# TensorE's increments and the waits on its products in the edge stage of a graph attention kernel

## The reference

```
h          = einsum('ni,hio->hno', layernorm(x), W)
edge_attn  = leaky_relu(attn_src[:, src] + attn_dst[:, dst], 0.2)
exp_attn   = exp(edge_attn - max(edge_attn))
attn_sum   = segment_sum(exp_attn, dst)
out        = segment_sum(exp_attn / (attn_sum[dst] + 1e-10) * h[:, src], dst)
x          = x + layernorm(x) + out
```

## Time and profile before

| | us |
|---|---|
| median of 3 runs | 1986.72 |
| lowest and highest | 1985.87, 1988.36 |
| the profiled execution, its own time | 1983.17 |
| its span | 1981.4 |

### The profile page before, as it was taken

One profiled execution on the slowest core, in us unless ns is written; L12 is line 12 of the kernel. 1 busy time (PEld: TensorE's weight loads), 2 busy tenths in 40 slices (PEclk: granted clock), 3 DMA queues, 4 the chain that ended last, 5 costly groups with the idle time before them and its releaser, 6 DMA issues.

```text
span 1981.4 us, 28027 instructions
## 1 busy us (share of the span) xinstructions
PE 1518.3 (77%) x6733; PEld 1113.7 (56%) x6733; DVE 1177.7 (59%) x3449; ACT 775.5 (39%) x2346; POOL 1213.1 (61%) x1197
## 2 busy tenths in 40 slices
PE   3927777777777777777777777673968999999975
PEld 2714444444444444444444444442848999999963
DVE  5746666666666666666666666668983444333338
ACT  2624444444444444444444444432622233223326
POOL 4066666666666666666666666645364776666757
PEclk9956666666666666766656666766559999999987
DMA  6544444444444444444444444432856878877876
GB/s 184 164 120 115 120 112 113 115 117 118 112 115 114 117 118 110 114 115 117 118 111 115 114 119 114 115 79 80 252 168 184 226 212 210 213 210 203 217 170 200
DMA packets 166686, 284.19 MB, mean 143 GB/s; under 512 B 31760, under 2 KB 93285, under 8 KB 166373
## 3 DMA queue, kind: packets, MB, share of 16 engines
q0 software_dynamic: 62256, 143.99, 30.5%
q1 hardware_dynamic: 101908, 137.90, 21.9%
q10 hardware_dynamic: 2368, 0.52, 0.2%
HBM read 240.97 MB, written 42.16 MB: 143 GB/s over the span
## 4 chain that ended last, share of the span: by engine, by line
PE 63%; DVE 18%; issue 8%; DVEq 3%; another core or an unknown queue 3%; POOL 2%; DMA 1%; ACT 1%; ACTq 0%; POOLq 0%; SPq 0%
PE bank L1057 29%; PE bank L1198 10%; PE bank L1210 10%; DVE region L1518 4%; PE bank L1046 3%; PE bank L1082 3%; PE bank L990 2%; DVE z L1471 2%; DVE region L1516 2%; DVEq L494 2%; PE bank L1043 2%; POOL region L925 1%; DVE z L1478 1%; DVE z L1483 1%
## 5 line engine op out<-in xcount | busy, mean ns | idle before, releaser
L895 POOL DMA_INDIRECT region<-node_rows,region x832 | 790.5, 950 | 483.7 <-issue 222.7
L1057 PE MATMUL bank<-region 128*128 128x264 f32 x1664 | 746.7, 597 | 84.5 <-DVE region L1518 81.3
L1057 PEld LDWEIGHTS bank<-region 128*128 128x128 f32 x1664 | 440.5, 290 | 224.2 <-issue 138.4
L1518 DVE TENSOR_TENSOR region<-region,bank 128x264 f32 x728 | 311.5, 428 | 354.3 <-PE bank L1057 269.0
L748 ACT ACTIVATE neg_max<-bank 128x1 f32<-128x1 f32 x104 | 17.8, 171 | 723.1 <-PE bank L1082 593.6
L1504 DVE TENSOR_TENSOR region<-region,bank 128x512 f32<-128x512 f32 x416 | 265.9, 681 | 7.2 <-ACT bank L755 4.8
L738 ACT ACTIVATE region<-iota_row,region 128x128 f32<-128x128 f32 x832 | 262.7, 386 | 0.0
L822 ACT ACTIVATE region<-bank,b_col 128x128 f32<-128x128 f32 x452 | 129.0, 368 | 311.6 <-PE bank L1198 210.6
L971 POOL DMA_INDIRECT sum_rows<-region,row_u x113 | 180.0, 1593 | 111.5 <-DVE region L1938 45.2
L1198 PEld LDWEIGHTS bank<-region 128*128 128x128 f32 x1808 | 220.1, 192 | 6.3 <-issue 0.4
L1198 PE MATMUL bank<-region 128*128 128x128 f32 x1808 | 220.7, 275 | 0.2 <-issue 0.2
(11 more groups left out here) (246 smaller groups left out, 1618.4 us busy)
## 6 DMA issues: line engine op xcount, KB each, us to landing
region<-in_L_ffn_w SPq DMA_DIRECT2D x129, 512.0 KB, 8.4
region<-dloc_rows SPq DMA_DIRECT2D x104, 256.0 KB
region<-node_rows,region POOLq DMA_INDIRECT x832
node_rows<-region SPq DMA_DIRECT2D x12, 528.0 KB
y_rows<-region SPq DMA_DIRECT2D x7, 896.0 KB, 5.5
sum_rows<-region SPq DMA_DIRECT2D x7, 896.0 KB, 7.7
region<-in_x SPq DMA_DIRECT2D x5, 896.0 KB, 12.4
region<-sum_rows SPq DMA_DIRECT2D x5, 896.0 KB, 11.1
```

Of the source, the lines that this page charges most:

```text
L895: p.indirect_dma_start(gathered[g % SLOTS][:, j, :], None, node_rows, bass.IndirectOffsetOnAxis(src_idx[:, k:k + 1], 0)).then_inc(row_in[g ...
L1057: pe.matmul(bank[AGG_BANKS[k % AGG]][:, 0:ROW], onehot[:, (g % 3) * GROUP + j, :], gathered[g % SLOTS][:, j, :], start=True, stop=True).th ...
L1518: v.tensor_tensor(rows, rows, new, ALU.add).then_inc(acc_add)
```

## The change

TensorE's increments are thinned out. Of the products of a turn only n = 1 and the last (n = 7) increment `agg_mm`, which makes two, and five with the transpose, the broadcast and the attention products. The last two turns have some more. TensorE completes matmuls in order, so a later signal also tells of earlier products: whoever waits for product 2 or 3 now waits for `zmax_tr`, for product 4 `max_bc`, for product 5 `ad_mm`, for product 0 the increment of product 1, and for product 6 that of product 7. This holds for VectorE's adds, GpSimd's gathers (product 1, 3, 5 or 7 of group g - 4, as j is 0, 2, 4 or 6), ScalarE's one-hots (product 7) and SyncE after the stage. VectorE leaves out a wait that equals the one before it. No computation is added or removed, and the order on each engine stays.

```diff
--- before.py
+++ after.py
@@ -1,4 +1,5 @@
 
+import itertools
 from contextlib import ExitStack
 
 import concourse.bass as bass
@@ -439,6 +440,24 @@
 
         def sums_of(g):
             return range(first_sum(g), first_sum(g + 1))
+
+        def signals_itself(k):
+            g, n = PLACE[k]
+            return n in (1, len(sums_of(g)) - 1) or (g == GROUPS and n in (3, 5)) or (g == GROUPS - 1 and n == 5)
+
+        PLACE = [(g, n) for g in range(GROUPS + 1) for n in range(len(sums_of(g)))]
+        OWN_SIGNALS = list(itertools.accumulate(int(signals_itself(k)) for k in range(STEPS)))
+
+        def product_done(k):
+
+            g, n = PLACE[k]
+            if g < GROUPS and n in (2, 3):
+                return zmax_tr, g + 1
+            if g < GROUPS and n == 4:
+                return max_bc, g + 1
+            if g + 1 < GROUPS and n == 5:
+                return ad_mm, g + 2
+            return agg_mm, OWN_SIGNALS[k] + int(not signals_itself(k))
         flat_parts = attn_parts[:, :, :, :].rearrange("p t k h -> p (t k h)")
 
         def z_bank(g):
@@ -598,7 +617,7 @@
             d.dma_start(sum_rows[TILES * P:(TILES + YB) * P, :].rearrange("(p r) (n f) -> p (r n) f", p=P, f=P),
                         ones[:, :].unsqueeze(1).broadcast_to([P, YB * F_IN // P, P])).then_inc(y_out[0], 16)
 
-            d.wait_ge(agg_mm, STEPS)
+            d.wait_ge(agg_mm, OWN_SIGNALS[STEPS - 1])
 
             def load_b2(e0, e1):
                 d.dma_start(b2_bc[:, e0 * F_IN:e1 * F_IN],
@@ -730,7 +749,7 @@
             def onehots(g):
 
                 if g >= 3:
-                    s.wait_ge(agg_mm, (g - 2) * GROUP)
+                    s.wait_ge(*product_done((g - 2) * GROUP - 1))
                 for half in range(2):
                     slot = (g % 3) * GROUP + half * 4
                     for j in range(4):
@@ -891,7 +910,7 @@
                 for j in range(GROUP):
                     k = g * GROUP + j
                     if g >= SLOTS and j % 2 == 0:
-                        p.wait_ge(agg_mm, (g - SLOTS) * GROUP + j + 2)
+                        p.wait_ge(*product_done((g - SLOTS) * GROUP + j + 1))
                     p.indirect_dma_start(gathered[g % SLOTS][:, j, :], None, node_rows,
                                          bass.IndirectOffsetOnAxis(src_idx[:, k:k + 1], 0)).then_inc(row_in[g % SLOTS], 16)
 
@@ -1054,8 +1073,10 @@
                     pe.wait_ge(weigh_ok, k // 2 + 1)
                     if k >= AGG:
                         pe.wait_ge(acc_add, k - AGG + 1)
-                    pe.matmul(bank[AGG_BANKS[k % AGG]][:, 0:ROW], onehot[:, (g % 3) * GROUP + j, :],
-                              gathered[g % SLOTS][:, j, :], start=True, stop=True).then_inc(agg_mm)
+                    ins = pe.matmul(bank[AGG_BANKS[k % AGG]][:, 0:ROW], onehot[:, (g % 3) * GROUP + j, :],
+                                    gathered[g % SLOTS][:, j, :], start=True, stop=True)
+                    if signals_itself(k):
+                        ins.then_inc(agg_mm)
             pe.wait_ge(xnt_ok, TILES)
 
             pe.wait_ge(rows_sb, 2 * STEP_BLOCKS)
@@ -1507,7 +1528,8 @@
                 g, j = k // GROUP, k % GROUP
                 if j == 0:
                     v.wait_ge(fall_ok, g + 1)
-                v.wait_ge(agg_mm, k + 1)
+                if k == 0 or product_done(k) != product_done(k - 1):
+                    v.wait_ge(*product_done(k))
                 if k >= 1:
                     v.wait_ge(acc_add, k)
                 rows = acc[:, bass.ds(tile * ROW, ROW)]
```

## The result

The changed kernel takes **1982.67 us** (median of 20 runs, 1980.67 to 1987.05), the kernel before, on the same chip, 1985.53 us (20 runs, 1983.43 to 1989.12). The ratio is 0.9987, with a 95% interval of 0.9981 to 0.9993: 0.13% less, which lies within the 0.2% that count as no change. 1966 had been forecast, 21 us less. What came true is the rival "only moved".

A forecast was written before the change was run, and what follows sets the result against it. GpSimd's loop of eight issues and one pause for held TensorE signals, 11.8 us a turn, was taken as the bound; 25 - 4 = 21 us off 1983.2 gives 1962, plus 3.55 for the median 1966, range 1930 to 2010.

The forecast's parts named there:

- only moved: Rival: the attention signal always waits for the drain or is never held; turn stays 11.78 us, 1987 to 1991 us; chance 0.19.
- A = 2.8: Assumed us from the start of TensorE's burst (products 6, 7, 0', 1', 2') to VectorE's add 5; gives a turn of 11.51.
- product 5 by the attention products' signal: VectorE's add 5 and GpSimd's fifth issue wait for the attention products; forecast gain 0.27 us a turn, 25 us over 94 turns.
- T = A + 8.71: Turn length in us: A from burst start to add 5, 1.62 to add 6, then 7.09 to the next burst.
- The GpSimd loop: Edge stage: eight gather issues take 9.7 us and one pause waiting for a TensorE signal 2.05, together 11.8 us a turn.
- Where the waits go: Sign: VectorE's long wait stands before add 5, GpSimd's before the fifth issue of eight, and add 6 follows without a wait.
- Six increments fewer: Part of the change on TensorE, priced at zero; the 26.3 ns rule would give an estimated 15 us over 94 turns.
- the hold goes: Rival: five increments are few enough, signals come as matmuls end, GpSimd never pauses; 165 us less, about 1820; chance 0.08.
- two pauses a turn: Rival: GpSimd pauses again before its seventh issue, 2 us more a turn, about 2175 us if in every turn; chance 0.25.
- The last turns: End of the edge stage, nine products a turn: add 6 waits two products longer; cost taken as 4 us.
- the hold: Reading that TensorE's increments around the burst are held while gathers run, coming about 1.9 us after GpSimd stops issuing.
- product 6 by product 7's signal: VectorE's add 6 waits for product 7; priced at nothing in the burst, 4 us at most in the last turns.

The follow-up runs named there:

- forced pause: Against base, GpSimd fills 768 unused columns and waits for that before the fifth gather of a group; 1991.01 us, base 1990.89 us.
- spread form: Against base, GpSimd fills 180 unused columns and waits for that before every gather from the fifth group on; 2015.63 us, base 1989.72 us.
- base: The kernel before plus run-time asserted bounds on the values the expert stage's scatters wait for; 1990.89 us, ratio 1.0033 in the first set.
- the fifth set: Runs of base, half of each row gathered, and 180-column fills before every gather, beside the kernel before, which took 1985.57 us.
- the sixth: Set of base (1784.73 us), the change with asserted bounds (1794.33) and 90-column fills before each gather (1932.47), beside the kernel before (1779.28).

## Why the prediction was wrong

**The failed step** is the value A = 2.8 for the part "product 5 by the attention products' signal". The prediction had shown that A = 3.07, a signal held until the gathers have drained, gives the turn of before to the digit, and then took 0.27 us less, on the argument that this signal is the first of those held and has fewer behind it. The trace shows 3.33 us from the burst's start to add 5 in the turn above (823.34 - 820.01), and a median of 3.40 over 84 turns. The pause there is 1.95, and over all turns as long as before. The 25 us of the sum are nothing, and the turn is 11.757 us, not 11.51. The other term of T = A + 8.71 was off as well: from add 5 to the next burst it is 8.34 us (median). With A = 3.40 the formula would have given 12.1; GpSimd's eight issues and its silence keep the turn at 11.76.

**Why no part of it could be had:** the wrong picture was of a signal with an age of its own. In the forced pause, the silence given early was taken off the pause to 0.03 us; in the spread form the pause was gone when each gap was 0.23 us longer. Both say that what has to be there is a sum of silence on GpSimd's side in each turn, about 1.75 us with eight issues, and not a date on TensorE's. With seven issues it was 1.65, so whether the sum is fixed or grows with the issues is open; the change has eight either way. Which of TensorE's signals GpSimd waits for only chooses where the silence is put. "The GpSimd loop does not care where its one pause is", said the prediction, and that sentence alone would have given the result.

**Right**, by its own steps:
- *The bound and the loop.* Eight issues and one pause, 11.78 us, held for the change and for half the bytes, and for the forced pause with its silence in two pieces. With seven gathers the turn was 0.1 us under seven issues and a whole pause.
- *Where the waits go.* VectorE's ahead of add 5, GpSimd's ahead of the fifth issue, add 6 without one. The forecast named the attention products as releaser; the profile says "remote". That it is their signal rests on the kernel with product 5's own, where the pause is back before the seventh issue.
- *Six increments fewer cost nothing.* Product 5 with a signal of its own (six increments instead of eleven, its wait where it was) is 0.07% over base, so the count gives no gain. By the Trainium skill ("TensorE: Matmul & The Clock Gate", The cost: per-tile semaphore tail), increments serialize at 26.3 ns each, an estimated 15 us here; no run shows them on the path.
- *The rivals "the hold goes" and "two pauses a turn"* had the smaller chances and did not come about: 92 waits of GpSimd in the change, 94 before.
- *The last turns*, in kind. The changed kernel is 2.0 us ahead at the burst before the last two turns (1321.4 against 1323.4) and 0.1 at the last product, so they cost 1.9 us where the sum took 4; adds 6 to 8 wait 1.22 us in one of those turns. Where nothing is held, the last turns cost 4.5 us:

```profile
1336.27 1.57 DVE L1540 TENSOR_TENSOR region<-region,bank 128x264 f32 x3 [1.22 <-PE bank L1076]
```

**Missed altogether:** that the hold isn't always there. Without it the change is a loss, 0.54% with all that belongs to it. The prediction took the hold as given, and so priced product 6 by product 7's signal at nothing in the main loop ("in the burst both come together"); without the hold they do not, and add 6 waits.

**The 0.13%** between the kernels is clear of noise (the interval ends at 0.9993), but it is no proof of a gain by fewer increments: base and the kernel with six increments differ by 0.07% in the other direction, and the turn's 0.014 us x 94 is 1.3 us. Its cause is open, and so is what in the chip holds the signals and why only in some sets. Every execution on record lists a span and a granted clock, so none is known to have run without the profiler; whether its recording has a part in the hold is open too.

## What to carry to other kernels

If an engine paces a loop with a fixed sum of work and silence, moving a wait to another signal moves the silence and saves nothing: first ask which sum the loop needs, and whether the edit takes something from it. A forced pause and spread gaps show how to ask: they give the silence elsewhere. Between "exactly as before" and a small gain by an unseen signal, the row with a number wins. Run the kernel before in more than one set before a stall is taken as a property of the program; a later signal in place of an earlier one (product 7's for product 6's) is a cost that such a stall can hide. And see which add waits before a wait is given a cause: the view of waits goes by line, and here it had all eight adds in one row.

## What the runs showed of the hardware

- **TensorE's semaphore signals reach VectorE and GpSimd late while GpSimd issues indirect gathers 1.254 us apart**, and come once GpSimd has been silent for some 1.75 us in all in a turn of eight issues (1.65 with seven); with 1.485 us between starts they come in time. Half the bytes change nothing, nor do the other queue's loads. That holds for four of the seven comparisons.
- **The hold is there in some sets and not in others.** The kernel before took 1984 to 1987 us in four comparisons (the first one and three sets) and 1778 to 1780 us in three sets, with turns of 11.77 us against 10.01 in base. It is not shown to be a property of the chip: the record gives the fifth set, which has the hold, and the sixth, which hasn't, the same chip number (9). What differs between them is not known.
